# VectorE's side work moved to other experts, and four weight transfers per batch instead of three, in the expert stage of a one-core kernel

## The chip, the cores and the metric

The kernel runs on one core of a Trainium2 chip. The metric is the device time of the whole program in microseconds (us). Five engines work side by side, each through its own queue in program order: TensorE (PE in the profile), VectorE (DVE), ScalarE (ACT), GpSimd (POOL) and SyncE (SP), which here only issues DMA transfers. They wait for one another by counting semaphores. A difference of 0.3% is about what a measurement of this kernel can tell from no change.

## The reference, cut to what matters

The input is `x`, 16 sequences of 512 tokens with 128 features. A gated linear attention with 8 heads comes first, then a layer norm, then a feed-forward part with 8 routed experts, 2 shared ones, and a second layer norm:

```python
x = _layernorm(x + attention(x))
h = _swiglu(x @ lin0_w + lin0_b, ...)                 # the head
scores = softmax(h @ gate_w.T)
topv, topi = top_k(scores, 4); topv = topv / sum(topv)
combine = zeros((t, 8)).at[arange(t)[:, None], topi].set(topv)
g = _silu(einsum('td,edh->eth', h, exp_w1)); u = einsum('td,edh->eth', h, exp_w3)
routed = einsum('te,etd->td', combine, einsum('eth,ehd->etd', g * u, exp_w2))
shared = _silu(h @ sh_w1) * (h @ sh_w3) @ sh_w2
h = _swiglu((routed + shared) @ lin1_w + lin1_b, ...) # the tail
out = _layernorm(x + h)
```

## The kernel before

The attention stage takes the first 1340 us and is not touched. Behind it the expert stage goes through the 16 sequences, called batches here, and within a batch through 10 experts, e = 0 to 9: the 2 shared ones first (e = 0 and 1), then the 8 routed ones. All products on PE are made of three passes over a high and a low part of each operand. There is no scheduler: every engine's order is written out in its `ffn` function, as a loop over e with side work hung on fixed values of e.

For expert e of batch n the chain is this.

- PE, `up(n, par, e)`: g and u, three matmuls each, into two pairs of PSUM banks. u of expert e waits until VectorE has finished `v_gu` of expert e - 2.
- ACT, `silu_expert`: sg = silu(g) (line 1112).
- VectorE, `gate_expert`: for a routed expert gu = sg x weights (line 1505; its output is named `kt_sb` for even e, `s_sb` for odd e), then gc = gu x u (line 1512, output `v_sb`). Line 1505 needs the combine weights of that expert on all 128 partitions (`cw`).
- ACT, `high_gc` (line 1119), then POOL, `low_gc` (line 505): the high and low part of gc.
- PE, `down(n, par, e)`, three experts later, adds to `r_ps`.

The side work of VectorE between two experts belongs to the next batch (n + 1) or to earlier ones (n - 1, n - 2):

- for batch n + 1: `head_x` (line 1428), `head_z` (line 1435), `head_xt` (line 1442), `logits`, then `rank_experts`, `finish_ranks` (lines 1479, 1481) and `choose` (lines 1487 to 1495), which end in `comb`, the combine weights of 512 tokens. PE turns `comb` (`weights_t`, line 834), ACT copies it to `comb_t` (line 1124), and SP writes it to DRAM and spreads each expert's row to all partitions (`spread_weights`, lines 387 to 405), before in three transfers.
- for batch n - 1: `low_r` (line 1447), on which `down(n, par, 0)` on PE waits, because both use one PSUM bank; `tail_z` (line 1517), whose output PE transposes in `tail_h` (line 868); and `ln2` (lines 1278 and 1281), the sum and the statistics for the second layer norm.
- for batch n - 2: `ln_variance` (lines 1287 to 1297) at e = 0. POOL makes `rstd` of it (`ln_rstd`, line 485), and `ln2_out` (line 1302) at e = 1 waits for it. SP stores the result.

Of the kernel before, what the change touches and what calls it, by code (L numbers as in the profile page):

```python
# [5 lines left out]
def gated_linear_attention_and_moe_block(  # L6
# [56 lines left out]
    B, T, D = x.shape  # L63
# [21 lines left out]
    with ctx:  # L85
# [3 lines left out]
        def sem(name):  # L89
            return ctx.enter_context(nc.semaphore(name))  # L90
# [162 lines left out]
        ct_out = sem("ct_out")  # L253
        cw_in = [sem(f"cw_in{i}") for i in range(2)]
        f_down = sem("f_down")
# [83 lines left out]
        def _(sp):  # L339
# [41 lines left out]
            def spread_weights(n):  # L381

                sp.wait_ge(a_ct, n + 1)
                if n > 1:
                    sp.wait_ge(cw_in[0], (n - 1) * 16)
                    sp.wait_ge(cw_in[1], (n - 1) * 32)
                sp.dma_start(cw_dram[n % 2], comb_t[:, :]).then_inc(ct_out, 16)
                if n == 0:

                    sp.wait_ge(e_lo, 3)  # L390
                    sp.wait_ge(qk_full, B * NP * STEPS)
                rows = cw_dram[n % 2]

                def to_all(lo, hi):

                    return bass.AP(rows.tensor, rows.offset + lo * T, [[0, 128], [1, (hi - lo) * T]])

                sp.wait_ge(ct_out, (n + 1) * 16)
                if n > 0:
                    sp.wait_ge(v_gu, (n - 1) * NE + NS + HE)  # L400
                sp.dma_start(cw_all[:, 0:HE * T], to_all(0, HE)).then_inc(cw_in[0], 16)
                if n > 0:
                    sp.wait_ge(v_gu, n * NE)
                sp.dma_start(cw_all[:, HE * T:(E - 1) * T], to_all(HE, E - 1)).then_inc(cw_in[1], 16)
                sp.dma_start(cw[E - 1], to_all(E - 1, E)).then_inc(cw_in[1], 16)

# [52 lines left out]
        def _(pool):  # L459
# [47 lines left out]
            def ffn(b, first=False):  # L507
                for par in range(2):
                    for e in range(NE):
                        low_gc(b + par, par, e)  # L510
                        if e == 0 and not first:
                            ln_rstd(B + b + par - 2)

            ffn(0, first=True)
            for i in range(1, B // 2):
                ffn(2 * i)
            ln_rstd(2 * B - 2)
            ln_rstd(2 * B - 1)
# [3 lines left out]
        def _(pe):  # L522
# [348 lines left out]
            def ffn(b, first=False, last=False):  # L871
                for par in range(2):
# [3 lines left out]
                    for e in range(NE):  # L876
                        up(n, par, e)

                        if e == 8 and has_next:
                            weights_t(n + 1)  # L880
# [45 lines left out]
        def _(act):  # L926
# [209 lines left out]
            def ffn(b, first=False, last=False):  # L1136
                for par in range(2):
# [3 lines left out]
                    for e in range(NE):  # L1141
# [18 lines left out]
                        if e == 5 and has_prev:  # L1160
                            tail_z(n - 1)
                        if e == 8 and has_next:
                            take_weights_t(n + 1)
# [19 lines left out]
        def _(dve):  # L1183
# [315 lines left out]
            def gate_expert(n, par, e):  # L1499
                k = n * NE + e  # L1500
                dve.wait_ge(a_sg, k + 1)
                if e >= NS:
                    half = (e - NS) // HE
                    dve.wait_ge(cw_in[half], (n + 1) * 16 * (half + 1))
                    nc.vector.tensor_tensor(gu[e % 2], sg[e % 2], cw[e - NS], ALU.mult).then_inc(v_mid, 1)  # L1505
# [23 lines left out]
            def ffn(b, first=False, last=False):  # L1529
                for par in range(2):  # L1530
# [3 lines left out]
                    for e in range(NE):  # L1534
# [70 lines left out]
```

## Time and profile before

| | us |
|---|---|
| median of 3 runs (lowest, highest) | 1857.27 (1854.2, 1860.64) |
| the profiled execution | 1858.47 |
| its span, from first to last instruction | 1856.8 |
| first expert-stage batch begins, about | 1350 |
| PE busy, PEld, DVE, ACT, POOL | 1694.0, 1405.9, 1464.1, 1080.0, 604.3 |

The span is what the profile's rows cover; the execution's time is 1.7 us more. Busy shares are means over both stages. In the expert stage matmuls overlap, so a busy PE row says little: starts 0.23 us apart are three-pass matmuls without a gap, starts 0.43 us apart are the same at the lower clock.

### The profile page before, as it was taken

The page shows a single profiled execution, that of the slowest core. Times are in us where ns is not written, and L with a number is a line of the kernel's source. Part 1 is how long each engine was busy: PE and PEld are TensorE (multiplying, and loading weights), DVE is VectorE, ACT ScalarE, POOL GpSimd, SP SyncE. Part 2 cuts the span into 40 slices and gives each one's busy share as a digit, 9 for nine tenths or more (in the row PEclk, how much of TensorE's full clock was granted, in tenths as well). Part 3 has the DMA queues.
Part 4 walks back from the last instruction along what each step waited for, and adds up shares of the span by engine and source line. Part 5 has one row for each costly group of instructions (what it writes and reads, how often), then busy time and mean ns, then how long its engine had stood idle before and what let it go on. Part 6 is the DMA issues. An engine that isn't in the chain of part 4 may idle for free.

```text
span 1856.8 us, 81545 instructions
## 1 busy us (share of the span) xinstructions
PE 1694.0 (91%) x35591; PEld 1405.9 (76%) x35591; DVE 1464.1 (79%) x3326; ACT 1080.0 (58%) x2352; POOL 604.3 (33%) x470
## 2 busy tenths in 40 slices
PE   6999999999999999999999999999788888888886
PEld 5787877878888788787887877887666766666764
DVE  4878887887888778787887877887667888887875
ACT  5665566566556656655665566566355555555553
POOL 3322222232222223222322322332134544444444
PEclk9999999999999999999999999999999999999998
DMA  7000000000000000000000000000031313131311
GB/s 211 4 9 9 4 9 4 10 4 9 10 4 10 4 9 4 9 10 3 9 4 10 4 9 9 4 9 4 8 103 58 115 57 115 58 114 58 115 52 63
DMA packets 35826, 60.80 MB, mean 33 GB/s; under 512 B 2825, under 2 KB 24593, under 8 KB 33425
## 3 DMA queue, kind: packets, MB, share of 16 engines
q1 hardware_dynamic: 35472, 55.59, 9.2%
q8 instruction: 283, 4.64, 1.1%
q14 instruction: 71, 0.57, 0.1%
HBM read 46.93 MB, written 4.46 MB: 28 GB/s over the span
## 4 chain that ended last, share of the span: by engine, by line
PE 74%; DVE 10%; issue 7%; ACT 6%; POOL 1%; DMA 1%; DVEq 0%; ACTq 0%; SPq 0%; POOLq 0%
PE bank L538 10%; PE bank L540 9%; PE bank L539 9%; PE bank L671 7%; PE bank L626 7%; PE bank L681 5%; PE bank L657 5%; PE bank L629 5%; PE bank L578 5%; PE bank L588 4%; PE bank L645 3%; PE bank L614 3%; ACT v_sb L971 2%; DVE k_sb L1302 1%; DVE kt_sb L1505 1%
## 5 line engine op out<-in xcount | busy, mean ns | idle before, releaser
L469 POOL TENSOR_TENSOR rn_sb<-ss_sb,expo 128x8 f32<-128x8 f32 x128 | 213.7, 1669 | 780.9 <-DVE ss_sb L1271 780.9
L1226 DVE TENSOR_TENSOR qq_sb<-qq_sb,tot_sb 128x512 f32<-128x512 f32 (+1 forms) x384 | 264.1, 688 | 187.3 <-PE bank L626 151.4
L1226 DVE TENSOR_TENSOR k_sb<-k_sb,tot_sb 128x512 f32<-128x512 f32 (+1 forms) x384 | 322.5, 840 | 3.5 <-PE bank L629 3.3
L996 ACT ACTIVATE at_sb<-diag_sb 32x256 f32<-32x256 f32 x256 | 106.0, 414 | 170.5 <-DVE diag_sb L1238 165.7
L971 ACT ACTIVATE v_sb<-bank,rn_sb 128x128 f32<-128x128 f32 x512 | 139.5, 384 | 82.4 <-PE bank L540 79.7
L626 PEld LDWEIGHTS bank<-qq_sb,k_sb 128*32 128x32 f32 x12288 | 128.7, 110 | 60.9 <-issue 46.8
L626 PE MATMUL bank<-qq_sb,k_sb 128*32 128x16 f32 x12288 | 149.8, 185 | 24.8 <-issue 23.5
L960 ACT ACTIVATE a_sb<-bank 128x512 f32<-128x512 f32 x128 | 76.5, 598 | 154.4 <-PE bank L540 145.9
L671 PE MATMUL bank<-v_sb,at_sb 128*128 128x128 f32 x1024 | 149.4, 289 | 4.8 <-DVE res L1278 2.5
L505 POOL TENSOR_TENSOR wq_lo<-v_sb,wq_hi 128x512 fp32r<-128x512 f32 x80 | 109.2, 1365 | 134.3 <-ACT wq_hi L1119 134.3
L505 POOL TENSOR_TENSOR wk_lo<-v_sb,wk_hi 128x512 fp32r<-128x512 f32 x80 | 108.9, 1361 | 129.5 <-ACT wk_hi L1119 129.5
L1112 ACT ACTIVATE sq_sb<-bank 128x512 f32<-128x512 f32 x160 | 95.6, 597 | 88.3 <-PE bank L540 84.9
L314 POOL TENSOR_TENSOR tot_sb<-a_sb 128x512 f32<-128x512 f32 x64 | 88.6, 1384 | 160.2 <-ACT a_sb L960 123.3
L538 PE MATMUL bank<-wg_hi,ew_hi 128*128 128x512 f32 x320 | 133.7, 418 | 4.6 <-DVE v_sb L1512 4.0
L671 PEld LDWEIGHTS bank<-v_sb,at_sb 128*128 128x128 f32 x1024 | 125.3, 192 | 10.0 <-issue 5.6
L629 PE MATMUL bank<-qq_sb,k_sb 128*32 128x32 f32 (+1 forms) x3072 | 121.3, 208 | 7.9 <-issue 6.8
L539 PE MATMUL bank<-wg_lo,ew_hi 128*128 128x512 f32 x320 | 128.3, 401 | 0.0
L540 PE MATMUL bank<-wg_hi,ew_lo 128*128 128x512 f32 x320 | 127.8, 399 | 0.0
L629 PEld LDWEIGHTS bank<-qq_sb,k_sb 128*32 128x32 f32 (+1 forms) x3072 | 104.3, 122 | 29.4 <-issue 15.7
L578 PEld LDWEIGHTS bank<-ones_wide,sq_sb 128*32 128x32 f32 x8192 | 83.1, 111 | 53.3 <-issue 43.9
L681 PE MATMUL bank<-s_sb,qq_sb 128*128 128x128 f32 x768 | 113.4, 284 | 3.2 <-DVE s_sb L1264 2.4
L578 PE MATMUL bank<-ones_wide,sq_sb 128*32 128x1 f32 x8192 | 96.3, 172 | 19.9 <-issue 18.5
(191 smaller groups left out, 4298.6 us busy)
## 6 DMA issues: line engine op xcount, KB each, us to landing
ew_raw<-cw_dram SPq DMA_DIRECT2D x16, 1024.0 KB, 4.8
ew_raw<-cw_dram SPq DMA_DIRECT2D x16, 768.0 KB, 5.4
x_nat<-in_L_attn_x_dram SPq DMA_DIRECT2D x16, 256.0 KB, 3.4
x_nat<-x_all SPq DMA_DIRECT2D x16, 256.0 KB, 2.5
e_sb<-cw_dram SPq DMA_DIRECT2D x16, 256.0 KB, 6.4
out_dram<-k_sb SPq DMA_DIRECT2D x16, 256.0 KB, 2.3
ew_raw<-in_L_ffn_exp_w_dram SPq DMA_DIRECT2D x3, 512.0 KB, 5.3
qq_sb<-in_L_attn_Wq_dram SPq DMA_DIRECT2D x1, 512.0 KB, 3.8
```

What stands on the lines that cost most here:

```text
L469: nc.gpsimd.tensor_tensor(rn_sb[par][:, i, :, :].rearrange("p h c -> p (h c)"), ss_sb[:, i * G:(i + 1) * G], expo[:, 0:G], ALU.pow).then_i ...
L505: nc.gpsimd.tensor_tensor(gc_part[1][(par * NE + e) % 4], gc[(par * NE + e) % 4], gc_part[0][(par * NE + e) % 4].bitcast(fp32), ALU.subtra ...
L538: nc.tensor.matmul(out_ap, stat(0), mov(0), start=start, stop=False)
L539: nc.tensor.matmul(out_ap, stat(0), mov(1), start=False, stop=False)
L540: return nc.tensor.matmul(out_ap, stat(1), mov(0), start=False, stop=stop)
L578: mm = nc.tensor.matmul((nb_ps, su_ps)[i][n * SB:(n + 1) * SB, col:col + 1], sq_sb[:, i * HP + h, lo:lo + SB], ones_wide[:, 0:1], start=Tr ...
L626: mm = nc.tensor.matmul(out[n * SB:(n + 1) * SB, g * HB:(g + 1) * HB], k_sb[par][:, left:left + SB], halves(qd_sb[par][:, left:left + SB], ...
L629: mm = nc.tensor.matmul(out[2 * m * n:2 * m * n + m, g * m:(g + 1) * m], k_sb[par][:, left:left + m], qd_sb[par][:, left + m:left + 2 * m] ...
L671: nc.tensor.matmul(y_ps[:, c * D:(c + 1) * D], at_sb[par][:, h * NC + c, :], v_sb[par][:, c, h * D:(h + 1) * D], start=p == 0 and h == 0 a ...
L681: mm = nc.tensor.matmul(y_ps[:, c * D:(c + 1) * D], qd_sb[par][:, lo:lo + C], s_sb[:, h, c - 1, :], start=False, stop=p == NP - 1 and h == ...
L971: last = nc.scalar.activation(v_sb[par][:, c, h * D:(h + 1) * D], pj[n][:, at:at + D], ACT.Copy, scale=rn_sb[par][:, 1, h, c:c + 1])
L1226: return nc.vector.tensor_tensor(view, view, by, ALU.mult)
```

## The change

Four edits, all in the expert stage.

1. VectorE's `ln_variance` of batch n - 1 now stands at e = 9 of batch n, behind that expert's `gate_expert`, and no longer at e = 0 of batch n + 1. `ln2` moves from e = 9 to e = 8. POOL's `ln_rstd` moves from e = 0 to e = 9.
2. VectorE's `tail_z` moves from e = 7 to e = 6, ahead of `gate_expert(7)`; `choose` moves from e = 6 to e = 7, behind it.
3. PE's `weights_t` and ACT's `take_weights_t` move from e = 8 to e = 9.
4. The combine weights come in four transfers: expert 2 alone, experts 3 to 5, 6 to 8, and 9. There are three semaphores for them.

```diff
-                sp.dma_start(cw_all[:, 0:HE * T], to_all(0, HE)).then_inc(cw_in[0], 16)
+                sp.dma_start(cw[0], to_all(0, 1)).then_inc(cw_in[0], 16)
+                sp.dma_start(cw_all[:, T:HE * T], to_all(1, HE)).then_inc(cw_in[1], 16)
                 if n > 0:
                     sp.wait_ge(v_gu, n * NE)
-                sp.dma_start(cw_all[:, HE * T:(E - 1) * T], to_all(HE, E - 1)).then_inc(cw_in[1], 16)
-                sp.dma_start(cw[E - 1], to_all(E - 1, E)).then_inc(cw_in[1], 16)
+                sp.dma_start(cw_all[:, HE * T:(E - 1) * T], to_all(HE, E - 1)).then_inc(cw_in[2], 16)
+                sp.dma_start(cw[E - 1], to_all(E - 1, E)).then_inc(cw_in[2], 16)
...
                         low_gc(b + par, par, e)
-                        if e == 0 and not first:
-                            ln_rstd(B + b + par - 2)
+                        if e == NE - 1 and not (first and par == 0):
+                            ln_rstd(B + b + par - 1)
...
-                        if e == 8 and has_next:
+                        if e == 9 and has_next:
                             weights_t(n + 1)
...
-                        if e == 8 and has_next:
+                        if e == 9 and has_next:
                             take_weights_t(n + 1)
...
-                        if e == 0 and not first:
-                            ln_variance(B + n - 2)
                         if e == 1 and not first:
                             ln2_out(n - 2, par)
...
                         if e == 6 and has_next:
                             finish_ranks(n + 1)
+                        if e == 6 and has_prev:
+                            tail_z(n - 1)
+                        if e == 7 and has_next:
                             choose(n + 1)
-                        if e == 7 and has_prev:
-                            tail_z(n - 1)
+                        if e == 8 and has_prev:
+                            ln2(n - 1)
                         if e == 9 and has_prev:
-                            ln2(n - 1)
+                            ln_variance(B + n - 1)
```

VectorE, from the ranks at e = 6 to the middle of e = 8, in the kernel before (`picked` to `comb` is `choose`, line 1517 is `tail_z`):

```order
L1481 TENSOR_REDUCE rank<-qq_sb 128x32 [waits v_top]
L1487 SCALAR_TENSOR_TENSOR picked<-rank,ex 128x32 [waits v_top]
L1490 TENSOR_REDUCE den<-picked 128x4 [waits v_top]
L1492 RECIPROCAL rden<-den 128x4 [waits v_top]
L1495 TENSOR_TENSOR comb<-picked,rden 128x32 [waits f_ct,v_top]
L1505 TENSOR_TENSOR s_sb<-sq_sb,ew_raw 128x512 [waits cw_in1,a_sg]
L1512 TENSOR_TENSOR v_sb<-s_sb,bank 128x512 [waits v_mid,p_gc,f_u]
L1517 SCALAR_TENSOR_TENSOR qq_sb<-bank,swf_b,qq_sb 128x512 [waits a_s2]
L1505 TENSOR_TENSOR kt_sb<-sq_sb,ew_raw 128x512 [waits cw_in1,a_sg]
```

The same place in the changed kernel, whose lines are numbered up to five higher:

```order
L1482 TENSOR_REDUCE rank<-qq_sb 128x32 [waits v_top]
L1522 SCALAR_TENSOR_TENSOR qq_sb<-bank,swf_b,qq_sb 128x512 [waits a_s2]
L1510 TENSOR_TENSOR s_sb<-sq_sb,ew_raw 128x512 [waits cw_in2,a_sg]
L1517 TENSOR_TENSOR v_sb<-s_sb,bank 128x512 [waits v_mid,p_gc,f_u]
L1488 SCALAR_TENSOR_TENSOR picked<-rank,ex 128x32 [waits v_top]
L1491 TENSOR_REDUCE den<-picked 128x4 [waits v_top]
L1493 RECIPROCAL rden<-den 128x4 [waits v_top]
L1496 TENSOR_TENSOR comb<-picked,rden 128x32 [waits f_ct,v_top]
L1510 TENSOR_TENSOR kt_sb<-sq_sb,ew_raw 128x512 [waits cw_in2,a_sg]
```

`tail_z` has moved ahead of expert 7, and `choose` behind it.

VectorE, from expert 9 to `ln2_out` at e = 1 of the next batch, in the kernel before:

```order
L1505 TENSOR_TENSOR s_sb<-sq_sb,e_sb 128x512 [waits cw_in1,a_sg]
L1512 TENSOR_TENSOR v_sb<-s_sb,bank 128x512 [waits v_mid,p_gc,f_u]
L1278 TENSOR_TENSOR res<-bank,x_all 128x512 [waits x1_done,f_hT]
L1281 BN_STATS stats<-res 128x6 [waits res_done]
L1281 BN_STATS stats<-res 128x6 x3
L1512 TENSOR_TENSOR v_sb<-sq_sb,bank 128x512 [waits p_gc,f_u,a_sg]
L1428 TENSOR_TENSOR xT_lo<-bank,xT_hi 128x512 [waits a_x1T]
...
L1297 TENSOR_TENSOR ve<-lt 128x4 [waits rstd_done,ln_chain]
L1512 TENSOR_TENSOR v_sb<-sq_sb,bank 128x512 [waits p_gc,f_u,a_sg]
L1302 TENSOR_SCALAR k_sb<-res,mean,rstd 128x128 [waits rstd_done]
```

The same place in the changed kernel:

```order
L1279 TENSOR_TENSOR res<-bank,x_all 128x512 [waits x1_done,f_hT]
L1282 BN_STATS stats<-res 128x6 [waits res_done]
L1282 BN_STATS stats<-res 128x6 x3
L1510 TENSOR_TENSOR s_sb<-sq_sb,e_sb 128x512 [waits cw_in2,a_sg]
L1517 TENSOR_TENSOR v_sb<-s_sb,bank 128x512 [waits v_mid,p_gc,f_u]
...
L1298 TENSOR_TENSOR ve<-lt 128x4 [waits rstd_done,ln_chain]
L1517 TENSOR_TENSOR v_sb<-sq_sb,bank 128x512 [waits p_gc,f_u,a_sg]
L1429 TENSOR_TENSOR xT_lo<-bank,xT_hi 128x512 [waits a_x1T]
L1517 TENSOR_TENSOR v_sb<-sq_sb,bank 128x512 [waits p_gc,f_u,a_sg]
L1303 TENSOR_SCALAR k_sb<-res,mean,rstd 128x128 [waits rstd_done]
```

The sum and the statistics stand one expert earlier, and the seven small instructions that end in `ve` stand between expert 9 and expert 0, with two gates and `xT_lo` between them and `ln2_out`.

## Rows read from the trace of the kernel before

**Rows 1.** PE timeline: first matmul of `down(n, par, 0)` in batches 1, 5, 15 (start, us).

```profile
1391.28 0.39 PE L538 MATMUL bank<-wk_hi,ew_hi 128*128 128x512 f32 x1
...
1514.62 0.47 PE L538 MATMUL bank<-wk_hi,ew_hi 128*128 128x512 f32 x1 [1.77 <-DVE wvo_lo L1447]
...
1820.89 0.77 PE L538 MATMUL bank<-wk_hi,ew_hi 128*128 128x512 f32 x1 [3.02 <-DVE wvo_lo L1447]
```

**Rows 2.** PE timeline, e = 8 and 9 of a batch with the lower clock.

```profile
1528.72 0.60 PE L834 MATMUL bank<-ident,comb 128*8 128x128 f32 x4 [1.35 <-DVE comb L1495]
...
1530.81 1.11 PE L868 MATMUL bank<-ident,qq_sb 128*128 128x128 f32 x4 [0.78 <-DVE qq_sb L1517]
...
1532.15 0.63 PE L539 MATMUL bank<-wg_lo,ew_hi 128*128 128x512 f32 x1
```

**Rows 3.** SP timeline: the DMA issues of three batches.

```profile
1501.16 0.28 SPq L387 DMA_DIRECT2D cw_dram<-comb_t  x1
1502.63 0.34 SPq L401 DMA_DIRECT2D ew_raw<-cw_dram  x1
...
1531.26 0.29 SPq L387 DMA_DIRECT2D cw_dram<-comb_t  x1
...
1562.75 0.28 SPq L387 DMA_DIRECT2D cw_dram<-comb_t  x1
```

**Rows 4.** DVE timeline, e = 6 to 8.

```profile
1525.25 0.69 DVE L1512 TENSOR_TENSOR v_sb<-kt_sb,bank 128x512 f32<-128x512 f32 x1
...
1527.06 0.95 DVE L1487 SCALAR_TENSOR_TENSOR picked<-rank,ex 128x32 f32<-128x32 f32 x1
...
1528.59 0.68 DVE L1505 TENSOR_TENSOR s_sb<-sq_sb,ew_raw 128x512 f32<-128x512 f32 x1
1529.40 0.69 DVE L1512 TENSOR_TENSOR v_sb<-s_sb,bank 128x512 f32<-128x512 f32 x1
1530.01 0.75 DVE L1517 SCALAR_TENSOR_TENSOR qq_sb<-bank,swf_b,qq_sb 128x512 f32<-128x512 f32 x1
```

**Rows 5.** DVE timeline, e = 0 to 3.

```profile
1507.89 1.27 DVE L1297 TENSOR_TENSOR ve<-lt 128x4 f32<-128x4 f32 x1
...
1510.36 2.09 DVE L1302 TENSOR_SCALAR k_sb<-res,mean,rstd 128x128 f32<-128x128 f32 x4 [0.60 <-POOL rstd L485]
...
1513.79 0.68 DVE L1447 TENSOR_TENSOR wvo_lo<-bank,wvo_hi 128x512 fp32r<-128x512 f32 x1
...
1515.04 1.42 DVE L1505 TENSOR_TENSOR s_sb<-sq_sb,ew_raw 128x512 f32<-128x512 f32 x1
```

**Rows 6.** POOL timeline beside rows 4 and 5.

```profile
1507.86 1.29 POOL L505 TENSOR_TENSOR wk_lo<-v_sb,wk_hi 128x512 fp32r<-128x512 f32 x1 [1.21 <-ACT wk_hi L1119]
1509.24 1.01 POOL L485 TENSOR_TENSOR rstd<-ve,expo 128x4 f32<-128x4 f32 x1
1510.50 1.35 POOL L505 TENSOR_TENSOR wk_lo<-v_sb,wk_hi 128x512 fp32r<-128x512 f32 x1 [0.25 <-ACT wk_hi L1119]
1514.61 1.30 POOL L505 TENSOR_TENSOR wq_lo<-v_sb,wq_hi 128x512 fp32r<-128x512 f32 x1 [2.75 <-ACT wq_hi L1119]
...
1526.69 1.27 POOL L505 TENSOR_TENSOR wq_lo<-v_sb,wq_hi 128x512 fp32r<-128x512 f32 x1 [0.39 <-ACT wq_hi L1119]
```

**Rows 7.** DVE timeline: operations of rows 4 and 5 beside an idle POOL.

```profile
1354.38 0.19 DVE L1487 SCALAR_TENSOR_TENSOR picked<-rank,ex 128x32 f32<-128x32 f32 x1
...
1814.16 0.17 DVE L1297 TENSOR_TENSOR ve<-lt 128x4 f32<-128x4 f32 x1
...
1842.12 1.11 DVE L1302 TENSOR_SCALAR k_sb<-res,mean,rstd 128x128 f32<-128x128 f32 x4 [1.20 <-POOL rstd L485]
```

**Rows 8.** DVE timeline, batch 0: the first routed expert.

```profile
1363.31 0.69 DVE L1505 TENSOR_TENSOR kt_sb<-sq_sb,ew_raw 128x512 f32<-128x512 f32 x1 [6.28 <-DMA ew_raw<-cw_dram]
```

**Rows 9.** Page, part 6: DMA issues, KB each, median us to landing.

```profile
ew_raw<-cw_dram SPq DMA_DIRECT2D x16, 1024.0 KB, 4.8
...
out_dram<-k_sb SPq DMA_DIRECT2D x16, 256.0 KB, 2.3
```

More of the change, by code:

```diff
@@ L253, in gated_linear_attention_and_moe_block @@
         ct_out = sem("ct_out")
-        cw_in = [sem(f"cw_in{i}") for i in range(2)]
+        cw_in = [sem(f"cw_in{i}") for i in range(3)]
         f_down = sem("f_down")
@@ L385, in spread_weights @@
                     sp.wait_ge(cw_in[0], (n - 1) * 16)
-                    sp.wait_ge(cw_in[1], (n - 1) * 32)
+                    sp.wait_ge(cw_in[1], (n - 1) * 16)
+                    sp.wait_ge(cw_in[2], (n - 1) * 32)
                 sp.dma_start(cw_dram[n % 2], comb_t[:, :]).then_inc(ct_out, 16)
@@ L516, in _ @@
                 ffn(2 * i)
-            ln_rstd(2 * B - 2)
             ln_rstd(2 * B - 1)
@@ L1502, in gate_expert @@
                 if e >= NS:
-                    half = (e - NS) // HE
-                    dve.wait_ge(cw_in[half], (n + 1) * 16 * (half + 1))
+                    if e == NS:
+                        dve.wait_ge(cw_in[0], (n + 1) * 16)
+                    elif e < NS + HE:
+                        dve.wait_ge(cw_in[1], (n + 1) * 16)
+                    else:
+                        dve.wait_ge(cw_in[2], (n + 1) * 32)
                     nc.vector.tensor_tensor(gu[e % 2], sg[e % 2], cw[e - NS], ALU.mult).then_inc(v_mid, 1)
@@ L1570, in _ @@
             ffn(B - 2, last=True)
-            ln_variance(2 * B - 2)
             ln2_out(B - 2, 0)
```

## The prediction

> **What bounds the kernel now.** Start with the PE timeline. `down(n, par, 0)` starts at 1391.28 us in batch 1 and at 1820.89 us in batch 15, 14 batches later [rows 1]: 429.6 us, 30.69 us a batch. The DMA issues of line 387, one a batch, lie 30.10 and then 31.49 us apart [rows 3], so there are short and long batches. The table of waits then names where PE stands, and the timeline gives the sizes: once a batch 1.77 us for `wvo_lo` (`low_r`) ahead of that `down` [rows 1], 1.35 us for `comb` at e = 8, and behind it 0.78 us for `tail_z` [rows 2]. The long batches are the ones where PE comes out of these last two waits (1.35 and 0.78 us, 0.7 us of work between) at the lower clock: `tail_h` takes 1.11 us and a matmul 0.63 us instead of 0.39 to 0.40 [rows 2]; the granted clock has fallen to 1.2 GHz. A long batch costs 31.49 - 30.10 = 1.4 us more. So the stage is bound by VectorE's queue at two points, e = 8 and e = 3, and between them by PE itself.
>
> Last, VectorE's durations beside POOL's. `ve`, 4 elements per partition, takes 1.27 us from 1507.89 [rows 5] while POOL runs 1507.86 to 1509.15 [rows 6]; beside an idle POOL it takes 0.17 [rows 7]. `picked` takes 0.95 us, from 1527.06 to 1528.01 [rows 4], POOL's operation ends at 1527.96 [rows 6]; alone it takes 0.19 [rows 7]. The four of line 1302 take 2.09 with POOL at 1510.50, between the first and second of them, and 1.11 alone [rows 5 to 7]. Line 1505 at 1515.04 takes 1.42 instead of 0.68, POOL ends at 1515.91 [rows 4 to 6]. So some VectorE instructions are held until POOL's ends; lines 1512 and 1447 never are. The Trainium skill ("SBUF — State Buffer", "Who interferes with whom") says the same as a rule: a VectorE instruction with two SBUF inputs, or in a two-port mode, and a GpSimd instruction that reads SBUF take one lock, for the whole instruction, and whoever is first keeps it. By the rule it is the phase against POOL and not the instruction that sets the price, so a move can also run into POOL; without it every moved piece would cost the same as before, and the sum for a batch would lose 1.9 us of its gains (`ve` and `picked`) and have none of the new blocks below.
>
> **The change part by part, by re-timing one steady batch.** Nothing moves ahead of 1525.25, where VectorE gates expert 6 [rows 4]. I use VectorE's spacings from start to start: line 1505 to 1512 0.81, line 1512 to the next 0.61 (1528.59, 1529.40, 1530.01), `choose` 1528.59 - 1527.06 = 1.53 blocked [rows 4], 0.76 less where `picked` is free [rows 4, 7].
>
> *`tail_z` first, `choose` behind expert 7.* Ranks end at 1527.06, `tail_z` (0.75 us, its input is made at e = 5) follows at once and is done at 1527.8; line 1505 of expert 7 is ready at 1527.72 and held to 1527.96 [rows 6], so its 1512 starts 0.68 after that, at 1528.64, as behind the block at 1515.91 (next start 1516.59). `choose` runs 1529.24 to 1530.00, free of POOL: 0.77 us saved. PE: after `up(8)` (over at 1528.72 - 1.35 = 1527.4) it does `down(5)` and `tail_h` at once, then g of expert 9; u waits for expert 7's gate (done 1529.33), and `weights_t` at 1530.1 waits for nothing. The two waits of rows 2 shrink from 1.35 + 0.78 to some 0.4 us. PE starts the next batch 1.5 us earlier than in a short batch.
>
> *`ln2` at e = 8, `ln_variance` at e = 9.* Gate of expert 8 at 1530.82, sum and statistics (an estimate of 1.5 us by their 0.68 and 4 x 0.22) to 1532.93. Between the end of a gate and POOL's low part lie 0.75 us (1525.94 to 1526.69 [rows 4, 6]), so POOL runs 1532.25 to 1533.54 and holds line 1505 of expert 9: its gate starts at 1534.22. This is a new block, 0.5 us. The variance chain (seven small instructions, 1.89 us with the blocked `ve`, 0.80 without) takes 1534.82 to 1535.62, with `ve` at 1535.51, 0.14 us ahead of POOL's next (1535.65): `ve` 0.17 instead of 1.27, 1.1 saved, but by a hair; if it is caught, `ve` costs 1.27 as now and the order of what follows shifts with it. Gate 0, `xT_lo`, gate 1: 1535.62 to 1537.42.
>
> *`rstd` and `ln2_out`.* POOL's `rstd` is queued behind the low part of expert 9 (to 1536.94) and takes 1.01 [rows 6]: done 1538.04. So the wait of 0.60 us stays. Two low parts (experts 0 and 1) are by then queued behind it, where now there is one that comes 0.25 us late [rows 6]. The first holds all of `ln2_out` to 1539.42. POOL has shown that it gets in between two instructions of line 1302 (1510.36, 1510.50 [rows 5, 6]), so I take the second to hold the remaining three: line 1505 of expert 2 at 1541.65. Bounds of this step: not held a second time, 1540.45; held for both and `ve` caught as well, about 1542.1.
>
> *`low_r` and the period.* From there 0.81 + 0.61 to `low_r` and 0.83 from its start to PE's `down(n, par, 0)` (1513.79 to 1514.62 [rows 1, 5]): 1543.90, against 1514.62 a batch before. The period is **29.28 us** (bounds 28.08 and 29.7). From `down(n, par, 0)` to expert 6 PE has no gap and the rest hangs on it as now. Its own work is a short batch less its waits, 30.10 - 1.77 - 1.35 - 0.78 = some 26 us, no limit. Gain 30.69 - 29.28 = 1.41 us, 14 times: **19.7 us**.
>
> *The clock.* This period has no low-clock stretch in it: the two waits close together are gone. What is left is PE's wait at e = 3, which grows from 1.77 to about 2.6 us, since PE comes earlier. 1.77 never lowered the clock, 3.02 did: 0.77 us for the first matmul [rows 1]. Unknown from 0 to 0.7 us a batch (every second one at 1.4); I take 0, as the row nearest in kind is the 1.77, and keep the other end for the range.
>
> *Four transfers.* In batch 0 VectorE waits 6.28 us for the first 1024 KB [rows 8], which take 4.8 [rows 9]; 256 KB take 2.3 [rows 9], so the wait shrinks by 2.2 to 2.5. Expert 3's 768 KB come when the 1024 did plus one more issue of 0.4 us, 0.3 to 0.4 us after the 1363.31 at which they now come, while line 1505 of expert 3 now starts two spacings and a `head_z` (0.81 + 0.61 + 0.65) after it, at 1365.4: 1.8 us gained. With about 0.8 us at e = 8 of batch 0 (only PE's wait, nothing of `ln2` there) **2.6 us**. In later batches the copy of `comb_t` now waits behind expert 8's high part: 1532.1 to 1532.65 (0.57 us each, an estimate), write 1532.7, 1.47 us to the next issue [rows 3], 1534.2; with 2.3 us it is there at 1536.5, with the 4.8 of the big one at 1539, and it is wanted at 1541.65. Hidden, 2.6 us to spare. The extra issue on SP holds up only SP; the store and the `x_nat` load come many us before their use.
>
> *The end.* Low clock behind the 3.02 us wait of the last batch goes (six matmuls at 0.43 instead of 0.23 us, 1.2 us), and the last `ln_variance` with it (0.2): **1.4 us**.
>
> Sum: 19.7 + 2.6 + 1.4 = 23.7 us. The profiled execution of before is 1858.47, 1.2 above the median of 1857.27; from the former it gives 1834.8, at the level of the median 1833.6. I say **1834 us**.
>
> **The rivals.** (a) One block only: POOL's second low part doesn't get in between `ln2_out`'s four. Period 28.08, 14 x 2.61 + 4.0 = 40.5 us, **1817**. For it: no row shows two low parts queued there; against it: the gap at 1510.50. (b) The low clock comes back at e = 3: period + 0.7, and 1.2 less at the end: 14 x 0.71 + 2.8 = 12.7 us, **1845**. For it: the wait is longer than any steady one; against it: half of the present pairs of 2.1 us don't lower it. (c) No change, within 0.3%: `ve` caught and the clock as in (b), period 30.4: 14 x 0.3 = 4, some **1852**. (d) Slower: POOL pile-up on VectorE. With 10 low parts of 1.29 us and ten two-input instructions of VectorE in 29 us, two more blocks of 1.3 us at e = 0 to 2 take the period to 31.9: 14 x 1.2 = 17 us lost, less 2.6: **1871**. It decides from 1.4 us of extra blocks a batch on. Against it: whoever is held shifts, and then meets POOL idle. A transfer later than 9 us for expert 2 would do the same; the slowest row is 4.8.
>
> **How the numbers follow.** Forecast 0.5, (a) 0.25, (b) 0.15, (c) 0.06, (d) 0.04. The forecast's own range, from its bounds, is 1826 to 1842. The range 1815 to 1848 takes in (a) and (b) and leaves out about 2 in 10, with what lies below (a). Measurements of this kernel tell 0.3%, 5.6 us, from no change. Faster than 1851.7: forecast, (a), (b) and a part of (c), 0.92; same 0.05; slower 0.03.
>
> **What would show it.** Right: DMA issues of line 388 about 29.3 us apart and all alike; PE's wait for `comb` gone, under 0.5 us; `ve` at 0.16 us, `picked` at 0.19; `ln2_out` at 3 us or more; the wait for `wvo_lo` at 2 to 2.8 us with the clock at 2.4 GHz. Wrong: the issues at two alternating distances (b); `ve` still at 1.27; a wait of VectorE for `ew_raw` in batches after 0; PE's wait for `v_sb` of expert 7 or 9 above 1 us, which would mean that the moved pieces have only pushed the wait one expert on.

## The result, and the profile after

| | before | after |
|---|---|---|
| median, lowest to highest (runs), us | 1858.95, 1854.2 to 1861.94 (4) | 1831.2, 1827.28 to 1834.53 (4) |
| profiled execution, its span, us | 1858.47, 1856.8 | 1834.5, 1832.7 |

The ratio is 0.9852, interval 0.9817 to 0.9887: 27.8 us faster by the medians. The forecast was 1834 us in a range of 1815 to 1848, so the measured 1831.2 lies in it, 3 us under the forecast.

A total hides what a stage did. The attention stage is the same code in both kernels, but it took a different time in each execution. VectorE's timeline of before and then of after, the last residual sum of that stage:

```profile
1339.44 0.69 DVE L1278 TENSOR_TENSOR res<-bank,x_all 128x512 f32<-128x512 f32 x1 [2.59 <-PE bank L681]
```

```profile
1345.48 0.69 DVE L1279 TENSOR_TENSOR res<-bank,x_all 128x512 f32<-128x512 f32 x1 [2.59 <-PE bank L682]
```

So I measure the expert stage from that row's start to the end of the span: 1856.8 - 1339.44 = 517.4 us before, 1832.7 - 1345.48 = 487.2 after. **The change is worth 30.2 us there**, and 6.0 us of it were lost in the stage that nobody touched. Over all profiled executions of this study, one for each kernel, that row starts between 1333.32 and 1345.85. Below, "the stage" is the expert stage so measured.

VectorE's timeline after, from the ranks at e = 6 to expert 3 of the next batch; it answers to [rows 4, 5]:

```profile
1523.22 0.74 DVE L1522 SCALAR_TENSOR_TENSOR qq_sb<-bank,swf_b,qq_sb 128x512 f32<-128x512 f32 x1
1523.88 0.93 DVE L1510 TENSOR_TENSOR s_sb<-sq_sb,ew_raw 128x512 f32<-128x512 f32 x1
1524.94 0.69 DVE L1517 TENSOR_TENSOR v_sb<-s_sb,bank 128x512 f32<-128x512 f32 x1
1525.54 0.18 DVE L1488 SCALAR_TENSOR_TENSOR picked<-rank,ex 128x32 f32<-128x32 f32 x1
...
1529.24 1.17 DVE L1510 TENSOR_TENSOR s_sb<-sq_sb,e_sb 128x512 f32<-128x512 f32 x1
...
1531.84 0.16 DVE L1298 TENSOR_TENSOR ve<-lt 128x4 f32<-128x4 f32 x1
...
1534.35 3.01 DVE L1303 TENSOR_SCALAR k_sb<-res,mean,rstd 128x128 f32<-128x128 f32 x4 [0.52 <-POOL rstd L487]
1537.27 0.68 DVE L1510 TENSOR_TENSOR kt_sb<-sq_sb,ew_raw 128x512 f32<-128x512 f32 x1
1538.08 0.69 DVE L1517 TENSOR_TENSOR v_sb<-kt_sb,bank 128x512 f32<-128x512 f32 x1
1538.69 0.68 DVE L1448 TENSOR_TENSOR wvo_lo<-bank,wvo_hi 128x512 fp32r<-128x512 f32 x1
...
1539.95 1.41 DVE L1510 TENSOR_TENSOR s_sb<-sq_sb,ew_raw 128x512 f32<-128x512 f32 x1
```

`picked` (0.95 before) and `ve` (1.27 before) are free. In their place expert 9 is held (1.17 instead of 0.67) and `ln2_out` takes 3.01 instead of 2.09. POOL's timeline beside it, answering to [rows 6]:

```profile
1528.56 1.30 POOL L507 TENSOR_TENSOR wk_lo<-v_sb,wk_hi 128x512 fp32r<-128x512 f32 x1 [0.42 <-ACT wk_hi L1120]
1531.97 1.30 POOL L507 TENSOR_TENSOR wk_lo<-v_sb,wk_hi 128x512 fp32r<-128x512 f32 x1 [2.11 <-ACT wk_hi L1120]
1533.22 1.01 POOL L487 TENSOR_TENSOR rstd<-ve,expo 128x4 f32<-128x4 f32 x1
1534.20 2.55 POOL L507 TENSOR_TENSOR wq_lo<-v_sb,wq_hi 128x512 fp32r<-128x512 f32 x2
```

The two low parts stand behind `rstd` without a gap. The view of line 1303 in that window shows what they do to `ln2_out`'s four instructions (duration of the shortest, median and longest, ns):

```profile
L1303 DVE TENSOR_SCALAR k_sb<-res,mean,rstd x4: 338/787/1334, 1534.3 to 1537.0; 128x128 f32<-128x128 f32 x4
```

Four of them take 1.11 us alone [rows 7]; here two are held for about one low part each. PE's timeline after, from e = 8 of the same batch, and at the end `down(n, par, 0)` of batch 15, answering to [rows 1, 2]:

```profile
1526.48 0.60 PE L835 MATMUL bank<-ident,comb 128*8 128x128 f32 x4
...
1531.28 0.50 PE L539 MATMUL bank<-wg_hi,ew_hi 128*128 128x512 f32 x1 [0.28 <-DVE v_sb L1517]
...
1539.52 0.47 PE L539 MATMUL bank<-wq_hi,ew_hi 128*128 128x512 f32 x1 [1.76 <-DVE wvo_lo L1448]
...
1798.31 0.47 PE L539 MATMUL bank<-wk_hi,ew_hi 128*128 128x512 f32 x1 [3.17 <-DVE wvo_lo L1448]
...
1799.46 0.63 PE L540 MATMUL bank<-wg_lo,ew_hi 128*128 128x512 f32 x1
```

The waits of 1.35 and 0.78 us are gone, the one at e = 3 stays. Behind the 3.17 us of batch 15 the matmuls take 0.63 instead of 0.39 us: the clock falls there as it did before. SP's timeline, answering to [rows 3]:

```profile
1500.35 0.29 SPq L388 DMA_DIRECT2D cw_dram<-comb_t  x1
1501.82 0.34 SPq L402 DMA_DIRECT2D ew_raw<-cw_dram  x1
...
1528.98 0.29 SPq L388 DMA_DIRECT2D cw_dram<-comb_t  x1
1531.79 0.33 SPq L402 DMA_DIRECT2D ew_raw<-cw_dram  x1
...
1557.62 0.29 SPq L388 DMA_DIRECT2D cw_dram<-comb_t  x1
```

The issues of line 388 lie 28.6 us apart in 12 of 13 steady batches (one is 29.8). Before, seven of 13 took 30.1 and six 31.5 to 31.7. The 29.8 is no matter of the clock but of a margin that the new order made smaller. Before, expert 8's gate starts 0.16 us ahead of POOL's low part (1530.67 and 1530.83). Now it follows `choose` and starts 0.06 us ahead (1526.31 and 1526.37), and once it came 0.15 us behind (1755.50 and 1755.35):

```profile
1755.50 1.68 DVE L1510 TENSOR_TENSOR kt_sb<-sq_sb,ew_raw 128x512 f32<-128x512 f32 x1
```

In every kernel below that has edits 2 and 3 and POOL's full low part, the gate of expert 8 is held once in this way, each time in the same batch.

### The profile page after: what moved, and what is told of

It is laid out like the page before. It is cut to its first block, busy times and chain, and to the rows that moved or that the text cites. A ratio compares the mean times of both kernels' runs of the same rounds, so it can differ in the third digit from the quotient of the medians.

```text
span 1832.7 us, 81575 instructions
## 1 busy us (share of the span) xinstructions
PE 1694.1 (92%) x35591; PEld 1403.5 (77%) x35591; DVE 1462.5 (80%) x3326; ACT 1076.9 (59%) x2352; POOL 605.3 (33%) x470
## 4 chain that ended last, share of the span: by engine, by line
PE 70%; DVE 12%; issue 8%; ACT 6%; POOL 2%; DMA 1%; DVEq 0%; SPq 0%; ACTq 0%; POOLq 0%
PE bank L539 9%; PE bank L672 8%; PE bank L541 8%; PE bank L540 8%; PE bank L627 7%; PE bank L682 5%; PE bank L658 5%; PE bank L630 5%; PE bank L579 5%; PE bank L589 4%; PE bank L646 3%; PE bank L615 3%; DVE v_sb L1517 2%; DVE kt_sb L1510 2%; ACT v_sb L972 2%
```

## The experiments

Stage lengths are of one profiled execution each, ratios are to the runs of the kernel before that were taken beside them. A stretch at the lower clock more or less, which differs between executions of one kernel, is 1 to 2 us of a stage.

| kernel | median, us | ratio (95%) | stage, us | steady distance of two batches, us |
|---|---|---|---|---|
| before | | | 517.4 | 30.1, six of 13 at 31.6 |
| after | 1831.2 | 0.9852 (0.9817 to 0.9887) | 487.2 | 28.6, one at 29.8 |
| dma_only | 1855.5 | 0.9986 (0.9964 to 1.0007) | 512.9 | 30.1, four of 13 at 31.6 |
| ln_only | 1840.52 | 0.9908 (0.9877 to 0.9939) | 500.8 | 29.7 |
| choose_only | 1835.77 | 0.9868 (0.984 to 0.9895) | 493.3 | 28.6, two longer |
| choose_no_pe | 1865.16 (one run) | | 529.1 | 30.5 to 33.3 |
| three_transfers | 1831.64 | 0.9844 (0.9806 to 0.9883) | 490.0 | 28.6, one at 29.8 |
| ln2out_e5 | 1801.13 | 0.969 (0.9658 to 0.9722) | 461.0 | 26.7, two of 13 at 28.0 |
| e5_copy_first | 1802.41 | 0.97 (0.9672 to 0.9729) | 459.5 | 26.7, one of 13 at 27.9 |
| choose_e5 | 1803.22 | 0.9741 (0.9705 to 0.9777) | 467.3 | 26.55, six of 13 at 27.9 |
| pool_short | 1783.8 (one run) | | 441.1 | 25.6, three longer |
| pool_memset | 1775.62 (one run) | | 440.6 | 25.6, four longer |

### Each edit alone

**dma_only**: the kernel before with edit 4 (the first diff block of the change), nothing else.

> The kernel before with the four transfers alone. Measure: the expert stage, from the last residual sum of the attention stage (start of res) to the end of the span, 517.4 us before and 487.2 with all edits; the attention stage, which no kernel here changes, differs by 6 us between those two profiles. Theory: only batch 0 gains, since the wait for expert 2's weights fell there from 6.28 to 5.24 us: expert stage 516 to 517 us, whole kernel within 2 us of before. Rival (the prediction's own size): 1.8 us or more, 515.6 or less. The periods stay as before, 30.1 and 31.5 us in turn.

The stage is 512.9 us, below my 516 to 517 and in the range that I gave the rival. But only 1.1 of the 4.5 us is the first distance (23.19 instead of 24.24); two long batches fewer, four instead of six, are about 3.1. Whether edit 4 has a part in that isn't shown. It needn't have: over 13 executions of the kernel before, the mean granted clock goes from 0.976 to 0.984 of full speed. The total can't be told from no change, so what is shown of edit 4 is the gain in batch 0.

**ln_only**: edit 1. VectorE's variance of batch n - 1 at e = 9, POOL's `rstd` with it:

```diff
-                        if e == 0 and not first:
-                            ln_variance(B + n - 2)
...
-                        if e == 9 and has_prev:
+                        if e == 8 and has_prev:
                             ln2(n - 1)
+                        if e == 9 and has_prev:
+                            ln_variance(B + n - 1)
```

> The kernel before with edit 1 alone: ln2 at e = 8, ln_variance and POOL's rstd at e = 9; choose, tail_z and weights_t stay. Theory (POOL's operations hold VectorE's, and PE's two waits at e = 8 are what lowers the clock): ve at 0.16 us saves 1.1 us a batch, but line 1505 of expert 9 and ln2_out are held longer, so the short batch stays near 30 us and the long ones of 31.5 remain, because PE still waits twice at e = 8: expert stage 505 to 514 us. Rival: what counts is only that 1.9 us of VectorE's work leaves the stretch ahead of low_r: 14 x 1.9 = 27 us, 491 us or less.

The stage gained 16.6 us, more than I gave it, because the long batches vanished. The low clock did not vanish: PE's timeline of this kernel, `tail_h` of one batch,

```profile
1494.25 1.12 PE L867 MATMUL bank<-ident,qq_sb 128*128 128x128 f32 x4 [0.78 <-DVE qq_sb L1516]
```

and the busy times of that stretch and of the next batch's (length, then PE, PEld, DVE, ACT, POOL; the granted clock stands third from the end):

```profile
1494.00:1498.00 4.00, 3.75 (x12) 3.16 (x13) 3.64 (x9) 1.78 (x4) 1.79 (x2) 0.57 0.26 59
1523.60:1527.60 4.00, 3.70 (x19) 3.14 (x20) 3.83 (x9) 2.11 (x5) 2.79 (x2) 1.00 0.24 90
```

Between 1400 and 1800 us `tail_h` waits 0.78 or 0.79 us in every batch of both kernels; the clock falls there in 3 of 14 here and in 6 of 13 before, and those are the six long ones. In this kernel a fall costs nothing: the batch of 1494 is 29.65 us long, as the others. VectorE's rows show where the time comes back. A batch at full clock has the gate of expert 9 at 1.63 us and `ln2_out` at 3.02:

```profile
1526.69 1.63 DVE L1504 TENSOR_TENSOR s_sb<-sq_sb,e_sb 128x512 f32<-128x512 f32 x1
...
1532.26 3.02 DVE L1301 TENSOR_SCALAR k_sb<-res,mean,rstd 128x128 f32<-128x128 f32 x4 [0.52 <-POOL rstd L485]
```

and in the batch with the low clock the same two, late by PE, no longer meet POOL's low parts in the same way:

```profile
1497.31 0.69 DVE L1504 TENSOR_TENSOR s_sb<-sq_sb,e_sb 128x512 f32<-128x512 f32 x1 [0.19 <-ACT sq_sb L1111]
...
1503.16 1.99 DVE L1301 TENSOR_SCALAR k_sb<-res,mean,rstd 128x128 f32<-128x128 f32 x4
```

The phase against POOL hands back about what the clock took (0.94 and 1.03 us against waits of 0.19 and, for `xT_hi`, 1.01), and PE's wait at e = 3 of 1.41 us, absent in this batch, takes the rest. The other two batches with a fall have the same rows (0.69 us for the gate, 1.98 and 2.00 for `ln2_out`). In the kernel before nothing is handed back: `ln2_out` is 2.09 in both kinds of batch, and VectorE waits 1.69 instead of 0.66 us for expert 9's `sq_sb`.

**choose_only**: edits 2 and 3, VectorE's part:

```diff
                             finish_ranks(n + 1)
-                            choose(n + 1)
-                        if e == 7 and has_prev:
+                        if e == 6 and has_prev:
                             tail_z(n - 1)
+                        if e == 7 and has_next:
+                            choose(n + 1)
```

> The kernel before with edits 2 and 3 alone: tail_z at e = 6, choose at e = 7, weights_t at e = 9; ln2 and ln_variance stay. Theory: picked at 0.19 us instead of 0.95, expert 9 gated about 1 us earlier, PE's waits at e = 8 gone and with them the stretches at the lower clock: all batches alike, about 29 us, expert stage 491 to 499 us. Rival: the batch is set by low_r alone, and what happens at e = 8 has slack ahead of it: 512 us or more, with PE's wait at e = 3 longer by what the wait at e = 8 lost.

These two edits give 24.1 of the 30.2 us, and the whole steady gain: 28.6 us a batch. VectorE's timeline shows the same stretch with the prices in other places:

```profile
1553.90 0.69 DVE L1512 TENSOR_TENSOR v_sb<-s_sb,bank 128x512 f32<-128x512 f32 x1
...
1561.77 1.26 DVE L1297 TENSOR_TENSOR ve<-lt 128x4 f32<-128x4 f32 x1
...
1564.21 2.09 DVE L1302 TENSOR_SCALAR k_sb<-res,mean,rstd 128x128 f32<-128x128 f32 x4 [0.60 <-POOL rstd L485]
...
1567.04 0.69 DVE L1512 TENSOR_TENSOR v_sb<-kt_sb,bank 128x512 f32<-128x512 f32 x1
```

From expert 7's gate to expert 2's: 1567.04 - 1553.90 = 13.14 us here, 1538.08 - 1524.94 = 13.14 in the changed kernel. Edit 1 frees `ve` (1.10 us), and expert 9 (+0.2) and `ln2_out` (+0.92) take it back. **On top of edits 2 and 3, edit 1 is worth nothing in a steady batch.** The 6.1 us between the two stages lie elsewhere: 2.2 in the first distance (26.87 against 24.65; edit 4 has 1.0 of it), 1.2 in the steady ones, where choose_only has one low stretch of the clock (30.21 us), and 2.6 behind the last issue of line 387, where its clock is low twice. The three single gains, 4.5, 16.6 and 24.1 us, add up to 45 and not to 30: the long batches, which each of edit 1 and edits 2 and 3 takes away, can be taken away once only.

**choose_no_pe**: choose_only without edit 3; PE's `weights_t` and ScalarE's copy back at e = 8:

```diff
-                        if e == 9 and has_next:
+                        if e == 8 and has_next:
                             weights_t(n + 1)
```

> The kernel before with edit 2 alone: `tail_z` ahead of expert 7 and `choose` behind it on VectorE; PE's `weights_t` and ScalarE's `take_weights_t` stay at e = 8. Theory: PE then meets `weights_t` before `choose` is done and stands there again, some 1.5 to 2 us, with `tail_h` and `down(5)` queued behind it, but VectorE's order sets the period, so that most of the gain of edits 2 and 3 stays: period 28.6 to 29.6 us. Rival: PE's order is what counts at e = 8, and without edit 3 the period is that of before, 30.1 us with long ones of 31.5 between; the expert stage then takes 510 us or more instead of the 493 with both edits.

My theory was wrong, and the rival too mild: the stage is 12 us longer than before, 4 of them in the first two distances and 6 in the thirteen steady ones. PE's timeline, `weights_t`, and then VectorE's gate of expert 9:

```profile
1529.34 0.60 PE L834 MATMUL bank<-ident,comb 128*8 128x128 f32 x4 [2.77 <-DVE comb L1495]
```

```profile
1532.44 0.69 DVE L1505 TENSOR_TENSOR s_sb<-sq_sb,e_sb 128x512 f32<-128x512 f32 x1 [1.73 <-ACT sq_sb L1112]
```

PE's queue is in order: `tail_h`, `down(5)` and g of expert 9 stand behind the 2.77 us, and VectorE then waits 1.73 us for that g. The same move of VectorE's is worth -24 us with edit 3 and +12 without it.

**three_transfers**: the changed kernel without edit 4.

> The changed kernel without edit 4: experts 2 to 5 again in one transfer. Theory: the steady period is the same 28.62 us, since VectorE waits for no weights there; batch 0 loses 1 us (wait 6.28 instead of 5.24) and batch 1, where VectorE waited 1.84 us for expert 2's weights even with its own transfer, another 0.5 to 1.2 us. Expert stage 488.5 to 490 us against 487.2 (both give or take one stretch at the lower clock, 1.2 us), whole kernel the same within the noise of the attention stage. Rival: later transfers collide in other batches too, 493 us or more.

490.0 against 487.2 us: the first distance is 25.67 instead of 24.65, the steady ones are equal. The other 1.8 us lie behind `down(n, par, 0)` of the last batch (36.2 against 34.4 us to the end), in code that both kernels share: this execution has a stretch at the lower clock there that the other hasn't, of which more below. So edit 4 gives 1 us in batch 0 and nothing behind it, as long as a batch is 28.6 us.

### What holds `ln2_out`

**pool_short**: the changed kernel, POOL's low part made for 64 of 512 columns only; the low part of the other columns is left out.

```diff
-nc.gpsimd.tensor_tensor(gc_part[1][...], gc[...], gc_part[0][...].bitcast(fp32), ALU.subtract)
+nc.gpsimd.tensor_tensor(gc_part[1][...][:, 0:64], gc[...][:, 0:64], gc_part[0][...][:, 0:64].bitcast(fp32), ALU.subtract)
```

> The changed kernel, POOL's low part (line 507) made for 64 of 512 columns only; the low part of the other columns of gc is left out. Theory (POOL's running instruction holds VectorE's): POOL's instruction falls from 1.29 to about 0.2 to 0.4 us, and with it every hold: ln2_out from 3.01 to some 1.1 to 1.6 us, line 1510 of experts 7 and 9 from 0.93 and 1.17 to 0.7, of expert 3 from 1.41 to 0.7; period 28.63 less 1.4 to 2.2, so 26.4 to 27.2 us. Rival (the long instructions are slow for a reason of their own, for instance what they follow): they keep their lengths and the period stays at 28.6 us.

**pool_memset**: the same instruction replaced by a zero fill of all 512 columns, which reads no SBUF; the low part of gc is left out.

```diff
-nc.gpsimd.tensor_tensor(gc_part[1][...], gc[...], gc_part[0][...].bitcast(fp32), ALU.subtract)
+nc.gpsimd.memset(gc_part[1][...].bitcast(fp32), 0.0)
```

> The changed kernel, POOL's low part of gc replaced by a fill with zero over the same 512 columns; the low part of gc is left out. It reads nothing from SBUF. Theory by the skill's rule (SBUF — State Buffer, Who interferes with whom): VectorE instructions with two SBUF inputs (line 1510, ve) are held only by a POOL instruction that reads SBUF, so line 1510 takes 0.69 us everywhere, also beside a running fill; the two-port tensor_scalar of line 1303 can still be held. Rival: any running POOL instruction holds them, in proportion to its length. The period shows nothing by itself, since the fill may be shorter than 1.29 us: the verdict is by the instructions that overlap a fill.

Both give 25.6 us a batch, below the 26.4 that I had as the least for pool_short. VectorE's timeline of pool_short, expert 8's gate, then `ln2_out`, then expert 2:

```profile
1506.78 0.68 DVE L1510 TENSOR_TENSOR kt_sb<-sq_sb,ew_raw 128x512 f32<-128x512 f32 x1
...
1513.72 1.11 DVE L1303 TENSOR_SCALAR k_sb<-res,mean,rstd 128x128 f32<-128x128 f32 x4
1516.03 0.69 DVE L1510 TENSOR_TENSOR kt_sb<-sq_sb,ew_raw 128x512 f32<-128x512 f32 x1 [1.20 <-DMA ew_raw<-cw_dram]
```

and POOL's of the same kernel, beside expert 8's gate and then free:

```profile
1506.85 0.79 POOL L507 TENSOR_TENSOR wq_lo<-v_sb,wq_hi 128x64 fp32r<-128x64 f32 x1 [2.54 <-ACT wq_hi L1120]
1509.03 0.32 POOL L507 TENSOR_TENSOR wk_lo<-v_sb,wk_hi 128x64 fp32r<-128x64 f32 x1 [1.39 <-ACT wk_hi L1120]
```

`ln2_out` is back at 1.11 us, and line 1510 of the odd experts takes 0.69 at most, so POOL's length was their price. The lock works the other way too: the gate began 0.07 us earlier, and POOL's 0.32 us became 0.79, ending with 0.18 us behind the gate. The zero fill shows neither; POOL's and VectorE's rows of pool_memset at the same place:

```profile
1498.72 0.53 POOL L507 MEMSET wq_lo<- 128x512 f32 x1 [2.35 <-ACT wq_hi L1120]
```

```profile
1498.68 0.68 DVE L1510 TENSOR_TENSOR kt_sb<-sq_sb,ew_raw 128x512 f32<-128x512 f32 x1
```

Both at their own length, side by side. It is so in all 94 places where a gate and a fill overlap, also in the eight where the fill began first and had 0.19 to 0.49 us to go: the gate takes 0.68 to 0.69, the fill 0.52 to 0.53. In the changed kernel 47 gates began behind a running low part, and they take 0.92 to 1.84. The Trainium skill ("SBUF — State Buffer", "Who interferes with whom") says that a VectorE instruction with two SBUF inputs contends with a GpSimd instruction that reads SBUF and not with one that only writes it; these rows agree. For `ln2_out` my expectation had left it open. It hardly shows a hold by a fill: in 13 batches it begins 0.30 us behind a fill's start and each of its instructions takes 0.34, in one it begins 0.16 us behind and the first takes 0.45.

In pool_short PE waits twice between 1400 and 1740 us, 0.55 and 0.36 for `wvo_lo`, in two of the longer batches. In a batch of 25.6 us it has no such wait: that is PE's own work, the floor for anything done on VectorE's queue.

### The version that beats both

**ln2out_e5**: the changed kernel with `ln2_out` at e = 5, where one low part has long ended and the next is not ready.

```diff
-                        if e == 1 and not first:
-                            ln2_out(n - 2, par)
...
                             rank_experts(n + 1)
+                        if e == 5 and not first:
+                            ln2_out(n - 2, par)
```

> The changed kernel with ln2_out moved from e = 1 to e = 5, behind rank_experts, where VectorE stands idle 1.27 us waiting for ScalarE. Theory: the 2.9 us of line 1303, held twice by POOL, are the last thing ahead of low_r on which down(n, par, 0) waits 1.76 us; at e = 5 they cost 1.1 us and fit in the idle time. Period 28.63 - 1.76 = about 26.9 us, PE without a wait at e = 3, expert stage 461 to 466 us, whole kernel about 1807. Rival: VectorE is the bound as a whole and the wait only moves to another place: period above 28, expert stage 480 us or more.

461.0 us, another 26 below the changed kernel. VectorE's timeline:

```profile
1505.33 1.11 DVE L1303 TENSOR_SCALAR k_sb<-res,mean,rstd 128x128 f32<-128x128 f32 x4
1506.68 0.69 DVE L1510 TENSOR_TENSOR kt_sb<-sq_sb,ew_raw 128x512 f32<-128x512 f32 x1 [0.24 <-ACT sq_sb L1113]
...
1521.52 1.76 DVE L1510 TENSOR_TENSOR kt_sb<-sq_sb,ew_raw 128x512 f32<-128x512 f32 x1 [1.73 <-DMA ew_raw<-cw_dram]
```

At e = 5 VectorE used to wait 1.27 us for `sq_sb`; `ln2_out` now fills 1.11 of that, so it costs next to nothing. What comes up next is the last row: the weights, here behind a late transfer, as SP's timeline shows ahead of that row:

```profile
1514.95 0.29 SPq L388 DMA_DIRECT2D cw_dram<-comb_t  x1
1517.80 0.33 SPq L402 DMA_DIRECT2D ew_raw<-cw_dram  x1
```

2.85 us from the write to the next issue, where 1.47 is usual, and 28.0 us from this write to the next batch's. The other long distance (1703.27 to 1731.20) has no such wait: there POOL is ahead of expert 8's gate, which takes 1.69 us from 1727.52, as in the changed kernel.

**e5_copy_first**: ln2out_e5 with ScalarE's copy of the turned weights ahead of the high part of expert 8.

```diff
+                        if e == 9 and has_next:
+                            take_weights_t(n + 1)
...
-                        if e == 9 and has_next:
-                            take_weights_t(n + 1)
```

> The kernel with ln2_out at e = 5, and ScalarE's copy of comb_t at e = 9 put ahead of high_gc of expert 8. In ln2out_e5 VectorE waits 14.0 us in 7 places for ew_raw, 5.5 of them in batch 0: with VectorE reaching expert 2 some 2.9 us earlier, the weights now come late in some batches. Theory: the copy runs about 1.5 us earlier (it waits for the gate of expert 8 now), the waits outside batch 0 and 1 go, and the expert stage falls from 461.0 by 0 to 4 us, since only a part of those waits reached PE (2 times 1.3 us for wvo_lo). Rival: the copy delays high_gc(8) and down(8) and gives back what it saves, 461 us or more.

VectorE waits for `ew_raw` behind batch 0 no more (8.5 us in six batches in ln2out_e5). The stage is 459.5 us, 1.5 less, and the first distance alone is 1.6 shorter; the totals, 1801.13 and 1802.41, can't be told apart. What is left between its 26.7 us and PE's 25.6 is seen on PE. It waits twice a batch, each time for the gate of an odd expert that POOL holds (expert 7 takes 0.94 us from 1510.22, expert 9 takes 1.16 from 1515.58). The second of the two:

```profile
1517.62 0.51 PE L539 MATMUL bank<-wg_hi,ew_hi 128*128 128x512 f32 x1 [0.30 <-DVE v_sb L1517]
```

With the first (0.21 us at 1512.03) and the slower starts behind each wait PE loses some 1.0 of the 1.1 us. VectorE's gate of expert 2 is held too, 1.76 us from 1520.63, but PE doesn't wait for it.

**choose_e5**: choose_only with `ln2_out` at e = 5, so without edits 1 and 4.

> The kernel before with edits 2 and 3 (`tail_z` ahead of expert 7, `choose` behind it, `weights_t` at e = 9) and with `ln2_out` at e = 5 behind `rank_experts`; `ln_variance` and `rstd` stay at e = 0, the weights come in three transfers. Theory: once `ln2_out` no longer meets POOL at e = 1, what edit 1 leaves is `ve`, held 1.1 us at e = 0, against a two-input gate of expert 9 that edit 1 puts in POOL's way (held 0.5 us): the period would be 26.7 + 0.6 = 27.3 us, the expert stage 461 + 14 x 0.6 + some 1 for batch 0, about 470, so the time about 1812. Rival: edit 1 is worth nothing here either, as on top of edits 2 and 3 without this move; period 26.7, time 1802 to 1804.

467.3 us is near my 470, but not by my reason; the time, 1803.22, and the short distance are those of the rival. VectorE's timeline, `ve` and expert 2:

```profile
1516.30 1.25 DVE L1297 TENSOR_TENSOR ve<-lt 128x4 f32<-128x4 f32 x1
...
1519.33 1.40 DVE L1505 TENSOR_TENSOR kt_sb<-sq_sb,ew_raw 128x512 f32<-128x512 f32 x1 [1.18 <-DMA ew_raw<-cw_dram]
```

Where VectorE waits 0.6 us or less for the weights a batch takes 26.55 us with `ve` held at 1.25, no more than the 26.7 with edit 1. Where it waits 0.85 to 1.56 us (1410, 1464, 1519, 1547, 1655 us) it is held by POOL on top (1.03 to 1.73 us), and the distance is 27.9; the sixth long one has the held gate of expert 8. So edit 1 is worth nothing here either. That the four transfers are what saves ln2out_e5 most of the long ones is my reading; a kernel with edits 1 to 3, three transfers and `ln2_out` at e = 5 was not run.

## Why the prediction was right, and where it was off

Its own three terms, against the two traces, with the marks it used (`res`, `down(n, par, 0)` of batches 1 and 15, the end):

| term | predicted gain | measured |
|---|---|---|
| 14 batches | 19.7 | 429.6 - (1798.31 - 1396.43) = 27.7 |
| batch 0 | 2.6 | (1391.28 - 1339.44) - (1396.43 - 1345.48) = 0.9 |
| the end | 1.4 | (1856.8 - 1820.89) - (1832.7 - 1798.31) = 1.5 |
| sum | 23.7 | 30.1 |

- **`tail_z` first, `choose` behind expert 7**: as re-timed. Expert 7's gate was held (0.93), `picked` was 0.18, PE's wait for `comb` fell to 3.9 us in all over 16 places.
- **`ve` and the new block at expert 9**: both came (0.16, and 1.17 instead of 0.67: 0.5 us). `ve` came by 0.13 us ahead of POOL (1531.84, POOL 1531.97), the hair that the text spoke of.
- **`ln2_out` held twice**: right in kind; 3.01 us against rival (a)'s one block. The size is what failed, the term "14 x 1.41". POOL's queued instructions follow one another without the gaps that I had put between them, and the second low part let a second `ln2_out` instruction in, so that two and not three were left: expert 2's gate starts 2.92 us after `ln2_out`, not 3.5. A steady batch is 28.63 us instead of 29.28, and the 14 intervals together are 8.0 us shorter than summed.
- **The wait at e = 3**: predicted to grow from 1.77 to 2.6 us, it stayed at 1.76. The batch is 0.65 us shorter than I had it, and PE now loses 0.21 and 0.28 us on VectorE's gates earlier in the batch.
- **The clock**: no low stretch in a steady batch after, as forecast, and the 1.77 us at e = 3 lowered it in no batch of either kernel, as read.
- **The end**: right by luck. The term took the low stretch behind the last batch's wait for gone (1.2 of its 1.4 us). It isn't gone. Behind the 3.17 us the granted clock is 0.50 from 1800 to 1802, and seven matmuls start 0.43 us apart, as six did behind the 3.02 [rows 1]; only the first three come before the fall. The 1.5 us measured are of another stretch: before, the clock is low again behind PE's last wait of 2.75 us for `wvo_lo`, from 1844.55 through the last `tail_h` (1.11 us for its four); after, that wait is 2.06 us and `tail_h` takes 0.66. From the last `low_r` to the last `res` that is 6.02 against 4.72 us. three_transfers has the same code there, a wait of 1.88 us and the low stretch, and 6.44 us; e5_copy_first has it behind the same 2.06 us as the changed kernel. So the length of a wait doesn't decide alone, nor does the pair at e = 8, which lowers the clock in some batches only. What decides stays open.
- **Four transfers**: oversized. Page, part 6, after, answering to [rows 9], and batch 0's wait, answering to [rows 8]:

```profile
ew_raw<-cw_dram SPq DMA_DIRECT2D x32, 768.0 KB, 6.3
...
ew_raw<-cw_dram SPq DMA_DIRECT2D x16, 256.0 KB, 3.7
```

```profile
1368.31 0.69 DVE L1510 TENSOR_TENSOR kt_sb<-sq_sb,ew_raw 128x512 f32<-128x512 f32 x1 [5.24 <-DMA ew_raw<-cw_dram]
```

The 256 KB at the head of a queue of 2 MB took 3.7 us, not the 2.3 of a store that runs alone, from which the term was priced: 1.0 us gained instead of 1.8. In batch 1 VectorE then waited another 1.84 us for `ew_raw`, where I had written that later batches hide the weights; three_transfers has 2.59 there, so that wait comes with the shorter batch 1 and not with edit 4. It is a part of why the term for batch 0, which ends at e = 3 of batch 1, measured 0.9 and not 2.6.
- **The total**: the profiled execution came out 24.0 us below the one before, against a sum of 23.7, and that is luck, because two errors met: the stage gained 6.4 us more than I summed, and the attention stage of the execution after was 6.0 us longer than that of before. The median of four runs is 27.8 lower, which is nearer to the stage than to my sum.

What the prediction didn't see at all is the shares: it priced all edits in one re-timing and could not have told that edit 1 adds nothing to edits 2 and 3 in a steady batch, and that edit 2 without edit 3 is a loss.

## What to carry to other kernels

Re-time a whole period on the queue that sets it, with every instruction at the phase at which it meets its rival for the lock; taking away one held instruction can be worth nothing, as edit 1 on top of edits 2 and 3, if the next ones arrive at a POOL instruction instead. Ask for each moved piece which other engine's queue has its consumer, and move both or neither. Look for the places where two engines arrive within a tenth of a us of each other: `ve` is free by 0.13 us and expert 8's gate by 0.06, and the latter was lost once in each profile. Put a block that can be held into a stretch where its engine waits anyway: that one move was worth nearly as much (26 us) as the four edits together (30).

## What the runs showed of the hardware

- With two POOL instructions that read SBUF queued against four short `ln2_out` instructions of VectorE, both engines get in by turns: 1.11 us alone, 2.09 with one, 3.01 with two.
- VectorE's gate holds POOL as well (0.32 to 0.79 us). Beside VectorE's gate a zero fill on POOL is neither held nor holds, in 94 overlaps.
- The time from SP's write to its next issue, which waits for the write, is 1.46 or 1.47 us in 15 of 16 batches before and 1.54 in the first. It is 2.81 and 2.59 for the weights of batches 6 and 7 in the changed kernel, 3.05 and 3.03 in the same two of three_transfers, 2.85 and 2.56 in those of ln2out_e5. Kernels with SP's write at its old place (dma_only, ln_only) and e5_copy_first, where it comes earlier again, stay at 1.55 or less. The cause was not tried.
- The granted clock of PE fell to half (1.2 GHz) in 6 of 13 batches before and in 3 of 14 of ln_only behind the same two waits, of 1.35 and 0.78 us with 0.7 us of work between. Of single waits, the 3.02, 3.17 and 3.58 us in the last batch of before, after and choose_only lowered it. One of 1.8 us at e = 3 did so in one batch of choose_no_pe and in none of before. One of 2.06 at the end of the program did so in e5_copy_first and not in the changed kernel.
